# Joining softmax halves by chunks, doubling and dividing TensorE work, and moving roots and row scaling to GpSimd in a two-layer attention block

## What is computed

```python
# layer 1: 16 heads of width 16; note the odd sums: the softmax is summed over m before v is used
x_proj = (x @ w_in.T + b_in).reshape(b, l, 16, -1)
q, k, v = jnp.split(x_proj, 3, axis=-1)
att = softmax(jnp.einsum('blhd,bmhd->blmh', q, k) * scale, axis=2)
opt = jnp.einsum('blmh,blhd->blhd', att, v).reshape(b, l, d)
x = layernorm(x + opt @ w_out.T + b_out)
# layer 2: 4 of 16 heads of width 64 are chosen by a router over the mean row
dist = softmax(mean(x @ Wr + br, axis=1));  idx = sort(top_k(dist, 4))
Qs, Ks, Vs = gather(x @ Wq + bq), gather(x @ Wk + bk), gather(x @ Wv + bv)
O = softmax(Qs Ks^T / 8) Vs
x = layernorm(x + O @ Wo + bo)
```

## Time and profile before

| | |
|---|---|
| time, median of 3 (lowest, highest) | 3965.09 us (3962.86, 3968.43) |
| the profiled execution: time, span of its trace | 3961.53 us, 3959.8 us |
| DVE, PE, ACT, POOL busy share of the span | 88%, 90%, 78%, 41% |
| mean granted TensorE clock | 0.911 of 2.4 GHz |

### The profile page before, as it was taken

How to read it: one execution, slowest core, us unless ns; L and a number is a source line. 1 busy time by engine, 2 the same in 40 slices (tenths; PEclk the granted TensorE clock), 3 DMA queues, 4 the chain that set the end, 5 groups by cost and what they waited for, 6 DMA issues and landing times.

```text
span 3959.8 us, 41484 instructions
## 1 busy us (share of the span) xinstructions
PE 3559.1 (90%) x13768; PEld 1260.7 (32%) x13768; DVE 3464.9 (88%) x3484; ACT 3097.4 (78%) x5053; POOL 1624.5 (41%) x1086
## 2 busy tenths in 40 slices
PE   7888888888999999799999999799999999799997
PEld 3233232232223232433322232333323232443333
DVE  7888889979999999879999999879999999667786
ACT  4888888867999999778999999678999999424333
POOL 3122233101444444423444444333444444737675
PEclk7677777679999999899999999799999999899998
DMA  5222222110000000200000000200000000100000
GB/s 161 69 74 71 74 75 73 55 52 17 17 17 27 17 27 17 83 23 12 27 17 27 17 27 16 87 22 17 27 17 27 17 27 1 56 7 12 11 11 11
DMA packets 117192, 142.60 MB, mean 36 GB/s; under 512 B 33394, under 2 KB 100466, under 8 KB 116978
## 3 DMA queue, kind: packets, MB, share of 16 engines
q1 hardware_dynamic: 116978, 139.95, 11.5%
HBM read 89.55 MB, written 50.33 MB: 35 GB/s over the span
## 4 chain that ended last, share of the span: by engine, by line
PE 42%; DVE 39%; ACT 14%; issue 3%; POOL 1%; SPq 1%; DMA 0%; DVEq 0%; POOLq 0%; ACTq 0%
DVE nmax L1185 26%; ACT ps L1003 13%; PE ps L962 10%; DVE smax L1264 9%; PE ps L865 8%; PE ps L830 6%; PE ps L844 6%; PE ps L927 5%; PE ps L942 5%; PE ps L977 1%; PE ps L838 1%; DVE y L721 1%; POOL facc L789 1%; DVE vals L1201 0%; PE ps L945 0%
## 5 line engine op out<-in xcount | busy, mean ns | idle before, releaser
L1003 ACT ACTIVATE ps<-ps,nmax 128x1024 f32<-128x1024 f32 x2048 | 2230.0, 1091 | 302.8 <-DVE nmax L1185 273.5
L1185 DVE TENSOR_REDUCE nmax<-ps 128x1 f32<-128x1024 f32 x2048 | 2382.3, 1215 | 95.3 <-PE ps L865 88.7
L865 PE MATMUL ps<-stack 96*128 96x512 bf16 x4096 | 1342.7, 426 | 206.3 <-ACT ps L1003 122.8
L789 POOL TENSOR_TENSOR facc<-facc,probs 128x1024 f32<-128x1024 f32 x443 | 1041.6, 2351 | 861.0 <-ACT probs L1090 776.4
L865 PEld LDWEIGHTS ps<-stack 96*128 96x128 bf16 x4096 | 280.5, 101 | 1373.9 <-ACT ps L1003 939.7
L1264 DVE TENSOR_REDUCE smax<-ps 128x2 f32<-128x1024 f32 x512 | 619.3, 1215 | 47.1 <-PE ps L927 47.0
L927 PE MATMUL ps<-fk,fq 64*128 64x512 f32 x2048 | 574.5, 644 | 63.1 <-ACT ps L1003 56.8
L942 PE MATMUL ps<-fq,fk 64*128 64x512 f32 x2048 | 548.4, 614 | 10.8 <-DVE probs L1294 5.5
L962 PE MATMUL ps<-probs,vals 128*64 128x512 f32 x2048 | 517.2, 612 | 4.4 <-ACT probs L1090 3.4
L1090 ACT ACTIVATE probs<-ps 128x1024 f32<-128x1024 f32 x384 | 389.2, 1015 | 26.7 <-PE ps L945 26.2
L1003 ACT ACTIVATION_READ_ACCUMULATOR ps<-ps,nmax 128x1 f32 x2048 | 409.0, 200 | 0.0
(11 more groups left out here) (127 smaller groups left out, 2035.6 us busy)
## 6 DMA issues: line engine op xcount, KB each, us to landing
stack<-qk_levels SPq DMA_DIRECT2D x768, 64.0 KB, 2.2
qk_levels<-fk SPq DMA_DIRECT2D x64, 384.0 KB, 2.6
probs<-in_L_attn_x SPq DMA_DIRECT2D x16, 512.0 KB, 3.8
res<-in_L_attn_x SPq DMA_DIRECT2D x16, 512.0 KB, 4.4
v_rows<-vals SPq DMA_DIRECT2D x16, 512.0 KB, 2.6
vrows<-v_rows SPq DMA_DIRECT2D x16, 512.0 KB, 3.4
x_rows<-y SPq DMA_DIRECT2D x16, 512.0 KB, 2.9
res<-x_rows SPq DMA_DIRECT2D x16, 512.0 KB, 3.8
```

What stands on the lines that cost most here:

```text
L789: pool.tensor_tensor(total, total, probs[:, slot, :], ALU.add).then_inc(facc_ready, 1)
L865: last = pe.matmul(bank(banks[i]), stack[0:SK, hd % 2, 0, t * P:(t + 1) * P], stack[0:SK, hd % 2, 1, col:col + CH], start=True, stop=True)
L1003: act.activation(src, src, ACT.Exp, bias=nmax[:, b % 2, half, t, hd:hd + 1], scale=-1.0, accum_out=esum[:, b % 2, half, t, hd:hd + 1]).the ...
L1185: dve.tensor_reduce(nmax[:, b % 2, half, t, hd:hd + 1], two_banks(banks), AX.XY, ALU.min).then_inc(min_ready, 1)
```

## The change

- **Join by chunks.** Chunk c of a batch is complete after A tile 487, 495, 503 or 511 (`CHUNK_LAST`), and its join is made then: DVE the smaller minimum, POOL the differences, ACT the exponentials (in place, in `nmax`), POOL the weighted sums, DVE the reciprocal, POOL `att` and `AT`. The buffer `joined` is gone. OT, OP and X1 of the first chunks stand among the last A tiles of their own batch, in a list of their own (`seam`).
- **The root** is a power of -0.5 on POOL (128 x 4 elements); the two ACT instructions and their table loads are gone. The scaling `NM` of the first three OP chunks of each batch runs on POOL too; the fourth, and those of the last batch's FO, on DVE.
- **Doubled tiles.** 378 of the 2048 A tiles (326 of them in batch 0) get each of their two matmuls twice, with the same result. `plan` picks an A tile for this when DVE has work queued and none of PE's last 12 units is an S, T, BC or V.
- **Divided projections.** A QP, KP, FK, FQ or D unit is issued in two parts, a VP, FV, OP or FO unit in four, and another unit can stand between the parts; when DVE has nothing queued, an A tile goes ahead of them.
- 20 tiles of the next batch ahead of a batch's layer 2 become 32; join, AT, OT, OP, X1 and RT units go first in ACT's, DVE's and POOL's queues; two layer-2 norms are moved past others; the splitting of the second half of batch 0's q goes from DVE to POOL (4 units).

```diff
+CHUNK_LAST = [A_TILES - HEAD_TILES + (c + 1) * TPC * HALF - 1 for c in range(NCH)]
-AHEAD = 20
+AHEAD = 32
+PARTS = {"QP": 2, "KP": 2, "FK": 2, "FQ": 2, "VP": 4, "FV": 4, "OP": 4, "FO": 4, "D": 2}
+PATIENT = {k: 20 for k in ("QP", "KP", "VP", "XT", "FK", "FQ", "FV", "OP", "FO", "OT", "X1", "D", "R", "RT")}
+    nm = lambda k, b, c: ((dve if k == "OP" and c + 1 == NCH or k == "FO" and b + 1 == B else pool)("NM", k, b, c))
-            split = dve if kind == "QP" and half[0] == 0 else pool
+            split = dve if kind == "QP" and half[:2] == (0, 0) else pool
+        done = [spot_a[b, j] for j in CHUNK_LAST]
+        seam += [(done[c], (kind, b, c)) for c, kind in ((0, "OT"), (0, "OP"), (0, "X1"), (1, "OT"), (1, "OP"))]
+        seam += [(done[c], (kind, b, c)) for c, kind in ((2, "OT"), (2, "OP"), (1, "X1"))]
+        rest = [("OT", b, 3), ("OP", b, 3), ("X1", b, 2), ("X1", b, 3), ("RT", b)]
...
+            if not queued and kind in PATIENT and at[4] < len(tiles):
+                spot, t = tiles[at[4]]
+                if pe(*t) in pe_ready and pick(2) and spot < best[0] + PATIENT[kind] / A_TILES:
+                    best = (spot, 4, pe(*t))
...
+                twice = n[1] == "A" and queued and not any(m[1] in mode for m in order["PE"][-NEAR:])
...
-                    for i in range(2):
+                    for i in (0, 1, 0, 1) if n in again else (0, 1):
...
+                elif kind == "J":
+                    if later == 0:
+                        pool.tensor_tensor(both, whole.unsqueeze(1).to_broadcast([P, HALF, TPC * AH]), both,
+                                           ALU.subtract).then_inc(comb, 1)
+                    else:
+                        pool.tensor_tensor(both, both, of_chunk(c, esum[:, b % 2, :, :, :]), ALU.mult).then_inc(comb, 1)
+                        pool.wait_ge(comb, base + 2)
+                        pool.tensor_tensor(whole, both[:, 0, :], both[:, 1, :], ALU.add).then_inc(comb, 1)
...
+                elif kind == "LN":
+                    pool.tensor_tensor(rstd[:, i % 2, :], var[:, i % 2, :], half_down[:, :], ALU.pow).then_inc(rstd_ready, 1)
...
-                elif kind == "LN":
-                    act.activation(rstd[:, i % 2, :], var[:, i % 2, :], ACT.Ln).then_inc(ln_ready, 1)
-                    act.wait_ge(ln_ready, i + 1)
-                    act.activation(rstd[:, i % 2, :], rstd[:, i % 2, :], ACT.Exp, scale=-0.5).then_inc(rstd_ready, 1)
```

More of the change, by code:

```diff
@@ L46 @@
 LEAD = "SAAAASAAAASAAAASAAAATTTTVVVV"
+PARTS = {"QP": 2, "KP": 2, "FK": 2, "FQ": 2, "VP": 4, "FV": 4, "OP": 4, "FO": 4, "D": 2}
+GAP = 0.6
+URGENT = ("J", "AT", "OT", "OP", "X1", "RT")
+PATIENT = {k: 20 for k in ("QP", "KP", "VP", "XT", "FK", "FQ", "FV", "OP", "FO", "OT", "X1", "D", "R", "RT")}
+PATIENT.update({"FK": 30, "FQ": 30})
+NEAR = 12
 def work_lists():
-    main, late, scores, products, inputs, tiles = [], [], [], [], [], []
+    main, late, scores, products, inputs, tiles, seam = [], [], [], [], [], [], []
     def place(units, start, span):
@@ L160, in fill @@
     def fill(tag, us, banks, after, read_by):
-        name = ("PE",) + tag
-        unit(name, us, after)
-        banks_of[name], reader[name] = banks, read_by
+        parts = PARTS.get(tag[0], 1)
+        for i in range(parts):
+            name = ("PE",) + (("part", i) if i + 1 < parts else ()) + tag
+            unit(name, us / parts, after if i == 0 else [])
+            banks_of[name] = banks if i == 0 else 0
+            if i == 0:
+                reader[name] = read_by
     pe = lambda *t: ("PE",) + t
@@ L332, in arrive @@
         else:
-            ready[n[0]].append((now, rank[n], n))
+            ready[n[0]].append((n[1] not in URGENT and n[2] != "OP", now, rank[n], n))
             queued += n[0] == "DVE"
@@ L364, in plan @@
                             best = (key, i, n)
+            kind = best and best[2][3 if best[2][1] == "part" else 1]
+            if not queued and kind in PATIENT and at[4] < len(tiles):
+                spot, t = tiles[at[4]]
+                if pe(*t) in pe_ready and pick(2) and spot < best[0] + PATIENT[kind] / A_TILES:
+                    best = (spot, 4, pe(*t))
             if best:
@@ L530, in build @@
         NEWTON_STEPS = 4
-        COMB_STEPS = 6
+        COMB_STEPS = 3
         ROUTE_STEPS = 11
         QK_DMAS, V_DMAS = 4 * FH // PAIRS, 2 * FH
-        order, held, freed, planned = plan()
-        fill_no = {n[1:]: i + 1 for i, n in enumerate(n for n in order["PE"] if n in held and n[1] != "V")}
+        order, held, freed, again, planned = plan()
+        fill_no = {n[1:]: i + 1 for i, n in enumerate(n for n in order["PE"] if n in held and n[1] not in ("V", "part"))}
         nth = {}
@@ L824, in _, with pieces, project_rows @@
             pe.wait_ge(wT_read, 3)
-            def project_rows(banks, rowsT, w):
-                for t in range(TPC):
+            def pieces(kind, piece, count):
+                parts = PARTS.get(kind, 1)
+                return range(count * piece // parts, count * (piece + 1) // parts)
+            def project_rows(kind, piece, banks, rowsT, w):
+                for t in pieces(kind, piece, TPC):
                     for cc in range(KC):
@@ L840, in transpose_rows, with project @@
                 last.then_inc(filled, 1)
-            def project(banks, wT, columns):
-                for cc in range(KC):
+            def project(kind, piece, banks, wT, columns):
+                for cc in pieces(kind, piece, KC):
                     last = pe.matmul(bank(banks[0]), wT(cc), columns(cc), start=(cc == 0), stop=(cc == KC - 1))
-                last.then_inc(filled, 1)
+                if cc == KC - 1:
+                    last.then_inc(filled, 1)
             for n in order["PE"]:
-                kind, at = n[1], n[2:]
-                banks = held.get(n)
+                if n[1] == "part":
+                    piece, kind, at = n[2], n[3], n[4:]
+                else:
+                    piece, kind, at = PARTS.get(n[1], 1) - 1, n[1], n[2:]
+                banks = held.get(("PE", kind) + at)
                 for was in freed.get(n, ()):
@@ L888, in _ @@
                     pe.wait_ge(oT_ready, b * NCH + c + 1)
-                    project_rows(banks, oT, w_outT)
+                    project_rows(kind, piece, banks, oT, w_outT)
                 elif kind == "X1":
@@ L913, in _ @@
                     pe.wait_ge(foT_ready, group_no(b, PAIRS * c + PAIRS - 1) + 1)
-                    project_rows(banks, foT(c), wo_sb)
+                    project_rows(kind, piece, banks, foT(c), wo_sb)
                 else:
```

166 lines of the change are left out of this document (90 added, 76 removed).

## The result

The changed kernel takes 3902.43 us (median of 4 runs, 3892.19 to 3926.99) against 3966.09 us (4 runs, 3962.86 to 3968.43): ratio 0.9851, 95% interval 0.9829 to 0.9874. It is faster by 64 us (59 by the ratio); forecast were 159, and the time lies 2 us outside the range. The profiled execution took 3895.25 us, its span is 3893.5.

The account below looks back on a forecast made before the run. DVE was taken to bound stage 0 and the first seam, PE the stretch from 3475 us on. Gains of 58 + 28 + 20 + 20 + 20 + 12 + 1.3 = 159 us gave 3806 us, range 3762 to 3900.

Parts of the forecast that it names:

- stage 0: Batch 0's A tiles with all projections between them (75 to 757 us): from 682 to 624 us, a gain of 58.
- woven stretches: The three stretches of A tiles woven with layer 2: 12 of DVE's 125.5 idle us gained, bounds 0 and 50.
- root as a power on GpSimd: Norms' root off ACT: one table load at the very end is on the path, 1.3 us gained.
- seams: Four stretches between the woven ones and after the last: less DVE work, shorter chain; gains 28, 20, 20 and 20 us.
- the first rival: Doubled tiles don't hold the clock and cost more than DVE's time: slower, 4010 us at 75% low clock; chance 0.08.
- stage 0's splits alone: Rival: stage 0 gains only its q splits, as the ring stops DVE; 46 us missing, 3852 us; chance 0.13.
- My last sentence: Failure sign: DVE's idle time between tiles grows while PE is waited for because of banks that ACT frees late.
- count nothing more: DVE's small instructions held up by GpSimd: one in six or so waits that long, so no further time was priced.
- The sum of 121 us: The gain if each of the 16 new two-input DVE minima waited up to 2.35 us for GpSimd, 38 us in all.
- seam 4: Last seam, a chain from fourth NM through X1, router and weights' transfer to the first FK: 20 us gained.
- GpSimd takes the seams' gain: Rival: NM stands before AT in GpSimd's queue, layer 2's additions behind; 88 us come back, 3894 us; chance 0.17.
- The power: Root of 128 x 4 elements on GpSimd: priced at 0.4 us, between 0.2 and 2.35.

Follow-up runs that it names:

- b_double_parts: The kernel before with doubled A tiles and divided projections, no join by chunks, roots on ScalarE, old planned costs: 3894.09 us, ratio 0.9825.
- b_double_parts_pow: The kernel before with doubled A tiles, divided projections and the root as a power on GpSimd, join as before: 3899.21 us, ratio 0.9838.
- a_costs: The changed kernel with the planner's three costs as before (A tile 0.437 us on PE, A tile and S 1.135 us on DVE): 3866.25 us, ratio 0.9756.
- k_dp_new: The kernel before with doubled tiles and divided projections, but the changed kernel's planned costs (0.47 on PE, 1.165 on DVE): 3919.58 us, ratio 0.9872.
- k_opt1: The changed kernel with old planned costs, and in batches 1 to 3 DVE's cost of A tile and S at 1.105 us: 3891.83 us, ratio 0.9812.
- a_parts1: The changed kernel with only QP and KP (in 2) and VP (in 4) divided, all other projections whole: 3900.83 us, ratio 0.9834.
- a_nmdve: The changed kernel with the scaling NM of each batch's third chunk back on DVE, next to the fourth's: 3936.13 us, ratio 0.9927.
- a_dve_more: The changed kernel with 48 more DVE minima of a tile in batches 1 to 3, into a buffer nobody reads: 3968.82 us, ratio 0.9999.
- k_opt2: The changed kernel with old planned costs, and in batches 1 to 3 DVE's cost of A tile and S at 1.05 us: 3838.42 us, ratio 0.9676.

## Why the prediction was wrong

The sum closes as a chain of kernels, each a step towards the change, by their ratios times 3966 us:

| step | forecast | measured |
|---|---|---|
| doubled tiles and divided projections (stage 0 and woven stretches) | 58 + 12 | 69 (before to b_double_parts) |
| root as a power on GpSimd | 1 | -5 (to b_double_parts_pow) |
| join by chunks, NM, seams, tiles ahead | 28 + 20 + 20 + 20 | 33 (to a_costs) |
| planned costs | not priced | -38 (to the change) |
| sum | 159 | 59 |

The measured column depends on the order of the steps. With the planned costs second, by k_dp_new, it reads 69, -19 for the costs, and 8 for the root, the join, NM and the seams together. Each difference has an interval of some 10 us beside it.

**Stage 0: right in its mechanism.** Clock 0.99, waits for VP gone, DVE idle 27.4 us. Its last tile comes 48 us earlier where 58 were forecast, and 56 with the old costs (701.9 us). That 69 stands beside 58 + 12 is in part luck: b_double_parts ends stage 0 63 us earlier and gains 22 up to the last tile of batch 3, and the stretch behind that is 21 us longer, of which I had nothing. The clock rule of the Trainium skill (TensorE: Matmul & The Clock Gate, A second HAM failure mode: psum-queue depth-cycling), by which the first rival would come, is not borne out there: doubled tiles go through the same ring at 0.99. But k_opt1 shows something of its kind in the woven stretch, where short pauses for PSUM banks stood ahead of a fall to 0.50 at 1154 us; the Trainium skill names the pattern, most such pauses here are followed by no fall, and the price of this fall is the 6 us of DVE work missing in those 14. The first rival (doubled tiles at the low clock) is refuted, as is stage 0's splits alone.

**The planned costs: the step that isn't in the sum.** I had looked at what the diff does to each instruction, and took three numbers changed by 8% and 3% as a recalibration without a price. They set the whole order. With a DVE believed faster, DVE mostly waits less for tiles, 175 to 119 us over the variants; from the change to a_costs, DVE is idle 12 us less and busy 11 us less between the last tiles of batches 0 and 3, and 8 us come in stage 0. That is 38 of the 100 us missing, or 19 by the other order of steps. My last sentence named a sign by which it would fail, and half of it came: DVE's idle time before A tiles grew (95.3 to 172.0 us), but PE's waits before them for banks that ACT frees did not (122.8 to 103.7 us).

**The seams: the terms 28, 20, 20, 20 were mis-sized,** 88 forecast and 33 measured with the old costs (8, with the root, at the new ones). The stretches from last tile to router did get 76 us shorter, near the 88. The step that failed is that I took this for a gain of the whole: 35 us of it came back between the routers and the next last tiles, and 23 behind the last router. First, the DVE work. I took 16.6 us a seam off DVE and wrote of contention that I "count nothing more". The join saved 17.4 us in all (35.5 to 18.1, near the 16 forecast) and the splits 13.1. NM went from 79.0 us to 50.6, 28.4 saved where 50.4 were forecast, as the 32 scalings left cost 12 us more than at their old mean; `var` alone, 13.0 to 31.2 us, ate 18.2. Its shortest, median and longest in ns are:

```profile
L1217 DVE TENSOR_SCALAR var<-mv x32: 169/598/1999, 687.5 to 3886.6; 128x4 f32<-128x4 f32 x32
```

Of the 32, 13 take over 1 us (3 of 32 before), where I had said one in six. They are those that GpSimd's additions of layer 2 overlap nearly from their start. The Trainium skill (SBUF — State Buffer, Who interferes with whom) says that tensor_scalar too can contend, in a mode that uses both ports; my sentence had taken from it the two-input instructions alone. `var` and the scaling are tensor_scalar with one tensor input, and they were held up here; whether they ran in that mode no run shows. The sum of 121 us was nearer than mine by luck: the 16 minima lost 6 us, not 38. This work isn't the whole loss either, as a_parts1 has 31 us less of it and is no faster beyond the noise. Second, the gain of seam 4 did not last. The chain there did get shorter (router 56.2 us behind the last tile instead of 80.4), but layer-2 matmuls that stood ahead of the router now stand behind it, where PE is the bound: PE is busy 33 us from last tile to router instead of 62, and 501 behind it instead of 477. From router to end it was 512.7 us and is 535.3, 22.6 given back. I had said that PE's work is left there as it was; a chain made shorter without less PE work doesn't end a PE-bound stretch earlier.

**GpSimd takes the seams' gain** (chance 0.17, 3894 us) gave nearly the measured time. That is in part luck, as it knew nothing of the planned costs. But its sign is there: the chain from last tile to router runs mostly on GpSimd in seams 2 to 4. Waits of PE in seam 4, 3240 to 3380 us:

```profile
PE ps L911 <- POOL vrows L815: 10.3, 1, 10.3
PE ps L911 <- DVE y L759: 8.8, 1, 8.8
PE ps L911 <- POOL y L759: 2.2, 1, 2.2
```

and the queue on POOL shows what AT (L815) stood behind, NM as I had feared:

```profile
3318.27 1.03 POOL L822 TENSOR_TENSOR rstd<-var,half_down 128x4 f32<-128x4 f32 x1
3319.28 2.34 POOL L858 TENSOR_TENSOR facc<-facc,probs 128x1024 f32<-128x1024 f32 x1
...
3322.72 4.83 POOL L759 TENSOR_SCALAR y<-y,mv,rstd 128x256 f32<-128x256 f32 x4
3327.52 0.32 POOL L811 TENSOR_TENSOR att<-att,nmax 128x64 f32<-128x64 f32 x1
3327.92 1.93 POOL L815 TENSOR_TENSOR vrows<-vrows,att 128x1024 f32<-128x1024 f32 x1
```

How much this costs is open. a_nmdve makes GpSimd's queue shorter and is 30 us slower; at the rate of a_dve_more its 33 us of DVE work would cost 35, so the shorter queue gave back about 5 at most. In a_parts1 the chain leaves GpSimd in seams 2 and 3, and the time stays. Neither changes the queue alone, as each has an order of its own.

**The power** takes 1.03 us, not 0.4, but within my bounds of 0.2 and 2.35. ACT's relief shows no gain of its own (5 us slower, within the noise); the 12 us that I had put to it and to dividing FV, FQ and FO together stand in the first row of the table.

What stays open: why an order planned for a faster DVE is faster, beyond the clock and the waits. One order, k_opt1, breaks the trend; a single order can be off it by some 20 us, as much as many terms of such a sum, and this holds for each step of the table too, since each has an order of its own. The split of the 33 us between join and NM wasn't measured, nor that of the lost seam gain between GpSimd's queue, its hold on DVE's small instructions and the moved work; NM on DVE for all chunks wasn't tried.

## What to carry to other kernels

Where a planner writes the order, its costs are part of the change: compare kernels with the same costs first, then sweep them, since here 0.03 us in three numbers is worth 38 us (19 without the join by chunks) and the best order found (k_opt2, 3838 us, 3.2% under the kernel before) differs from the changed one in those numbers alone. When work moves to GpSimd, look in the timeline where DVE's small instructions fall beside its wide additions: the same GpSimd work left `var` at 0.26 us in one order and at 0.97 in another. Count a shorter stretch as a gain only once it is clear that its work hasn't moved to another, and a shorter chain only up to the engine that bounds the stretch behind it. Before summing gains, test in which engine's time they are paid: added DVE work cost 1.07 us for each us here, added PE work some 0.3 (0 to 0.6 by its interval).
